# Two decay tiles in SBUF instead of PSUM, in a Mamba and mixture-of-experts kernel

## The reference, cut to what matters

```
dA = exp(dt * A[d, n])
h  = dA * h + dt * B[t, n] * x[t, d]
y[t, d] = sum over n of h[d, n] * C[t, n]
```

## Time and profile before

| | before |
|---|---|
| median of 3 runs | 3176.71 us (3176.48 to 3183.27) |
| the profiled execution | 3177.25 us |
| its span | 3175.4 us |
| mean granted TensorE clock | 0.877 |
| PE busy | 2478.4 us, 78% |
| DVE busy | 2488.7 us, 78% |
| ACT busy | 1384.3 us, 44% |
| POOL busy | 1709.0 us, 54% |

### The profile page before, as it was taken

One profiled execution on the slowest core, in us unless ns is written; L12 is line 12 of the kernel. 1 busy time (PEld: TensorE's weight loads), 2 busy tenths in 40 slices (PEclk: granted clock), 3 DMA queues, 4 the chain that ended last, 5 costly groups with the idle time before them and its releaser, 6 DMA issues.

```text
span 3175.4 us, 35516 instructions
## 1 busy us (share of the span) xinstructions
PE 2478.4 (78%) x10000; PEld 1482.7 (47%) x10000; DVE 2488.7 (78%) x3450; ACT 1384.3 (44%) x2258; POOL 1709.0 (54%) x1290
## 2 busy tenths in 40 slices
PE   5567676697869888697978879697987979687783
PEld 3344444454545455454544545454554545454441
DVE  1888888888888887888888888888978888887202
ACT  2453535354544445354444544354453545432221
POOL 1554656465655656565564756556564656555212
PEclk9778777898979989898998989898998989898987
DMA  2762432223223333333332333333333343333455
GB/s 68 260 241 89 136 103 78 80 93 100 84 80 110 121 99 114 113 107 113 103 120 90 127 106 113 105 101 117 111 112 103 115 128 99 94 113 124 158 185 186
DMA packets 187309, 373.15 MB, mean 118 GB/s; under 512 B 23024, under 2 KB 23024, under 8 KB 187120
## 3 DMA queue, kind: packets, MB, share of 16 engines
q1 hardware_dynamic: 146576, 263.91, 26.2%
q0 software_dynamic: 20480, 67.13, 6.3%
q10 hardware_dynamic: 20064, 39.85, 3.4%
HBM read 212.99 MB, written 157.81 MB: 117 GB/s over the span
## 4 chain that ended last, share of the span: by engine, by line
PE 42%; DVE 27%; issue 14%; POOL 8%; ACT 6%; DMA 3%; DVEq 0%; SPq 0%; POOLq 0%; ACTq 0%
PE work L1011 32%; DVE h L805 10%; DVE acc L819 7%; PE hT L1016 6%; POOL u L557 5%; DVE xc L843 2%; PE work L1016 2%; PE work L1064 2%; ACT decay L690 1%; DMA y_row<-result_scratch,rows_of 1%; DVE acc L816 1%; DVE xc L866 1%; ACT L690 1%; ACT sz L729 1%; DVE shift L884 1%
## 5 line engine op out<-in xcount | busy, mean ns | idle before, releaser
L557 POOL TENSOR_TENSOR u<-xc,b_ring 128x1024 f32<-128x1024 f32 x512 | 1205.0, 2357 | 1057.9 <-DVE h L805 787.0
L690 ACT ACTIVATE decay<-dt,neg_a 128x512 f32<-128x512 f32 x1024 | 705.8, 691 | 1048.9 <-DVE h L805 1035.4
L1016 PE MATMUL hT<-ident,h 128*128 128x128 f32 x4096 | 690.4, 308 | 441.7 <-DVE acc L819 298.3
L819 DVE SCALAR_TENSOR_TENSOR acc<-hT,ct,acc 128x512 f32<-128x512 f32 x960 | 700.2, 730 | 226.8 <-PE hT L1016 200.7
L1016 PEld LDWEIGHTS hT<-ident,h 128*128 128x128 f32 x4096 | 531.3, 158 | 687.7 <-DVE acc L819 388.4
L1011 PE MATMUL work<-w_exp,xeT 128*128 x1536 | 724.4, 616 | 26.7 <-issue 19.1
L805 DVE TENSOR_TENSOR_SCAN h<-decay,h_last,u 128x512 f32<-128x512 f32 x512 | 652.1, 1274 | 44.2 <-ACT decay L690 20.0
L805 DVE TENSOR_TENSOR_SCAN h<-decay,u 128x512 f32<-128x512 f32 x512 | 620.5, 1212 | 57.3 <-ACT decay L690 51.1
L1011 PE MATMUL work<-xnT,w_in 128*128 128x512 f32 x1024 | 476.9, 610 | 0.8 <-ACT xnT L705 0.8
L1011 PEld LDWEIGHTS work<-w_exp,xeT 128*128 128x128 f32 x1536 | 286.1, 196 | 347.1 <-issue 346.7
L1011 PEld LDWEIGHTS work<-xnT,w_in 128*128 128x128 f32 x1024 | 190.5, 196 | 201.3 <-issue 196.2
(11 more groups left out here) (143 smaller groups left out, 1914.6 us busy)
## 6 DMA issues: line engine op xcount, KB each, us to landing
b_ring<-b_scratch SPq DMA_DIRECT2D x256, 256.0 KB
xe<-row_scratch SPq DMA_DIRECT2D x180, 256.0 KB
result_scratch<-ye SPq DMA_DIRECT2D x180, 256.0 KB
row_scratch<-x_out ACTq DMA_DIRECT2D x32, 1024.0 KB, 4.8
xn<-in_x SPq DMA_DIRECT2D x64, 256.0 KB, 4.5
x<-in_x SPq DMA_DIRECT2D x64, 256.0 KB, 5.3
x_scratch<-x SPq DMA_DIRECT2D x64, 256.0 KB, 2.9
x_out<-x_scratch SPq DMA_DIRECT2D x56, 256.0 KB, 3.9
```

The lines of the kernel that those rows point to most:

```text
L557: nc.gpsimd.tensor_tensor(out=u[:, at:at + 2, :], in0=xc[:, half, 2 * k:2 * k + 2, :], in1=b_ring[:, n % ROWS:n % ROWS + 1, :].to_broadcas ...
L690: nc.scalar.activation(decay_bank[g % 2][:], dt[:, half, :], ACT.Exp, scale=neg_a[:, c, n:n + 1]).then_inc(decay_ready, 1)
L819: nc.vector.scalar_tensor_tensor(out=acc[:, q, :], in0=hT_bank[q % 2][:], scalar=ct[:, ip, q, m:m + 1], in1=acc[:, q, :], op0=ALU.mult, op ...
L1016: last = nc.tensor.transpose(ps[:, k * P:(k + 1) * P], tile(k), ident[:])
```

## The change

The two decay tiles are allocated in SBUF, 128 x 512 fp32 each, under the same names. The activation that writes them and the scan that reads them are the same lines with the same waits. The order list is written by another loop: one pass over all 64 places, with constants HT = 2 (number of hT banks) and LAG = 0 (places by which sums are put off), and the sums and transposes come from counts over the whole block. The numbers of the hT banks and the waits on them are written with those counts and have the same values.

The function `transposed_at` gives the transposes of a place. For the sums it yields the places of before. For the transposes of q = 2 and 3 too: behind the sums of q = 0 and 1. Those of q = 0 and 1 of state n come at place 4n + 3, behind its scan and sum and before its side steps; in the list of before they came after these side steps, at the head of state n + 1. For the last state of a block this is the end of the block's own list instead of the head of the next one's.

```diff
@@ -38,6 +38,8 @@
     WORK = 4
+    HT = 2
+    LAG = 0
@@ -122,6 +124,11 @@
+    def transposed_at(at):
+        def last(at):
+            return min(at - C - LAG + HT, (at + 1) // C * C - 1)
+        return range(last(at - 1) + 1, last(at) + 1)
@@ -144,25 +151,24 @@
-        for n in range(N):
-            m, blk = (N - 1, -1) if n == 0 else (n - 1, 0)
-            summing = tail if n == 0 else scan
-            if summing:
-                steps += [("h_T", m, 0, blk), ("h_T", m, 1, blk)]
...
-            for c in range(C):
-                if scan:
-                    steps += [("u", n, c // 2)] * (c % 2 == 0) + [("decay", n, c), ("scan", n, c)]
-                if summing:
-                    steps.append(("h_sum", m, c, blk))
-                    if c + 2 < Q:
-                        steps.append(("h_T", m, c + 2, blk))
...
-                steps += place[n * C + c]
+        for at in range(N * C):
+            n, c = at // C, at % C
...
+            if scan:
+                steps += [("u", n, c // 2)] * (c % 2 == 0) + [("decay", n, c), ("scan", n, c)]
+            k = at - C - LAG
+            if scan if k >= 0 else tail:
+                steps.append(("h_sum", k % (N * Q) // Q, k % Q, k // (N * Q)))
+            for t in transposed_at(at):
+                if scan if t >= 0 else tail:
+                    steps.append(("h_T", t % (N * Q) // Q, t % Q, t // (N * Q)))
...
+            steps += place[at]
@@ -304,8 +310,8 @@
-        decay_bank = [bank(f"decay{i}") for i in range(2)]
-        hT_bank = [bank(f"hT{i}") for i in range(2)]
+        decay_bank = [sb(f"decay{i}", [P, T]) for i in range(2)]
+        hT_bank = [bank(f"hT{i}") for i in range(HT)]
@@ -1024,8 +1031,9 @@
-                        wait(pe, summed, (i * N + m) * Q + q - 1)
-                        transposes(hT_bank[q % 2], lambda k: h[:, m % 2, k, q * P:(q + 1) * P]).then_inc(hT_ready, 1)
+                        k = (i * N + m) * Q + q
+                        wait(pe, summed, k - HT + 1)
+                        transposes(hT_bank[k % HT], lambda k: h[:, m % 2, k, q * P:(q + 1) * P]).then_inc(hT_ready, 1)
```

More of the change, by code:

```diff
@@ L146, in iteration @@
         steps = []
-        for n in range(N):
-            m, blk = (N - 1, -1) if n == 0 else (n - 1, 0)
-            summing = tail if n == 0 else scan
-            if summing:
-                steps += [("h_T", m, 0, blk), ("h_T", m, 1, blk)]
[L152 to L155, removed]
-            for c in range(C):
-                if scan:
-                    steps += [("u", n, c // 2)] * (c % 2 == 0) + [("decay", n, c), ("scan", n, c)]
-                if summing:
-                    steps.append(("h_sum", m, c, blk))
-                    if c + 2 < Q:
-                        steps.append(("h_T", m, c + 2, blk))
-                if scan and j % 2 == 0 and c == 1 and n > 0:
-                    steps.append(("keep_h", n - 1))
-                steps += place[n * C + c]
+        for at in range(N * C):
+            n, c = at // C, at % C
+            if c == 0:
+                if scan and n + 1 < N:
+                    steps.append(("load_b", n + 1, 0))
+                elif do_prep and n + 1 == N:
+                    steps.append(("load_b", 0, 1))
+            if scan:
[6 more added lines that the diff above has]
+                    steps.append(("h_T", t % (N * Q) // Q, t % Q, t // (N * Q)))
+            if scan and j % 2 == 0 and c == 1 and n > 0:
+                steps.append(("keep_h", n - 1))
+            steps += place[at]
         if scan and j % 2 == 0:
@@ L809, in steps_of @@
                         i, ip = j + blk, (j + blk) % 2
-                        dve.wait_ge(hT_ready, (i * N + m) * Q + q + 1)
+                        k = (i * N + m) * Q + q
+                        dve.wait_ge(hT_ready, k + 1)
                         if m == 0:
@@ L815, in steps_of @@
                                     wait_product(dve, j, ("y_T", C - 1))
-                            nc.vector.tensor_scalar(acc[:, q, :], hT_bank[q % 2][:], ct[:, ip, q, m:m + 1], None, ALU.mult).then_inc(summed, 1)
+                            nc.vector.tensor_scalar(acc[:, q, :], hT_bank[k % HT][:], ct[:, ip, q, m:m + 1], None, ALU.mult).then_inc(summed, 1)
                         else:
                             dve.wait_ge(summed, (i * N + m - 1) * Q + q + 1)
-                            nc.vector.scalar_tensor_tensor(out=acc[:, q, :], in0=hT_bank[q % 2][:], scalar=ct[:, ip, q, m:m + 1],
+                            nc.vector.scalar_tensor_tensor(out=acc[:, q, :], in0=hT_bank[k % HT][:], scalar=ct[:, ip, q, m:m + 1],
                                                            in1=acc[:, q, :], op0=ALU.mult, op1=ALU.add).then_inc(summed, 1)
```

## The result

The changed kernel takes 3580.97 us in the median (3575.23 to 3582.18, 4 runs) against 3176.6: 1.1264 times as long, with a 95% interval of 1.1245 to 1.1284, or +404 us. 3570 us were forecast, with a range of 3340 to 3760.

The account below looks back on a forecast made before the run. VectorE and TensorE were each busy 78% of the span, neither alone the bound. Terms 10 + 457 + 15 + 10 + 25 - 150 + 30 = +397 us on 3177 gave 3574, stated as 3570 us, range 3340 to 3760.

Parts of the forecast that it names:

- The write of decay: ScalarE writing the decay tile to SBUF: +15 ns each, at most 15 us, hidden while decays wait for the scan; taken as 0.
- The scan alone: VectorE's scan with both inputs in SBUF: 0 to +20 ns for each of 1024 scans; taken as +10 us.
- The scan stands still for the product: A scan with two SBUF inputs meeting GpSimd's u gets 0.18 us done, stands until u ends, then does the rest.
- How often: Scans meeting GpSimd work: +457 us for first scans during u, +15 gating products, +10 small gate operations, +25 later-starting u.
- the term of late products: 80 u that now start in a scan would start later, by up to 51 us in all, hitting the next scan: +25 us.
- Given back: VectorE's 200.7 us of waits for hT before sums shrink: -150 us; +30 for gaps that leave more of u uncovered.
- its two causes: Later scans make transposes less late; transposes q = 0 and 1 move ahead of TensorE's other steps; together 0 to -200.7 us.
- The sum: All terms added: 10 + 457 + 15 + 10 + 25 - 150 + 30 = +397 us.
- absorbed by 300 us: Rival 1: VectorE's stalls fall into 300 of its 407 us idle time; 3394 us, range 3300 to 3400; chance 13%.
- The convoy: Rival 2: late GpSimd makes u meet the gap inside pairs too, +549 us, nothing given back; about 3830 us; chance 10%.
- a scan that does not stand: Rival 3: the scan does not stand for GpSimd; 3119 us, faster than before; chance 5%.
- a slower TensorE: Lower TensorE clock delaying sums: taken as 0, with up to 50 us of idle time given back left as its price.

Follow-up runs that it names:

- e6: As e5 (u in 2 of 512 columns), with both decay tiles in SBUF, order of before: 3149.92 us, 0.9914 of the kernel before.
- e5: Kernel before, with GpSimd computing u in 2 of its 512 columns except in the first block's first two states: 3102.84 us, 0.9759.
- e3: Kernel before, with only the decay tile of each pair's first scan in SBUF, the second in PSUM: 3457.87 us, 1.0887.
- e4: Kernel before, with only the decay tile of each pair's second scan in SBUF, the first in PSUM: 3248.46 us, 1.0234.
- e7: Changed kernel with each 128x1024 product u as two 128x512 instructions, the scan waiting for the second: 3475.71 us, 1.0933 of the kernel before.
- e1: Changed kernel with both decay tiles back in PSUM, so only the new order of transposes: 3197.24 us, 1.0064 of the kernel before.
- e8: As e1, with a block's second c_project moved from place 39.7 to 38.9, ahead of the moved transposes: 3174.48 us, 0.999 of the kernel before.
- e2: Kernel before, with both decay tiles in SBUF and the order of before: 3569.2 us, 1.1241.
- e9: Kernel before (decay in PSUM, order of before) with each u as two products of 128x512: 3164.26 us, 0.9958.

## Why the prediction was right, point by point

- **The write of decay, 0 us.** The activation takes 721 ns in the mean against 691, +30 ns and not +15. That it is hidden fits the runs: e6, which has it too, is 47 us over e5 with 40 of them in the scans, so at most 7 are left for it.
- **The scan alone, +10 us.** The medians rose by 6 and 10 ns, about 8 us.
- **The scan stands still for the product.** Right in kind: 1.08 us after the product's end is near the 1.24 - 0.18 = 1.06 that the row add's 0.18 us gave. The 1.08 us are the same for scans that take 1.21 us alone and for those that take 1.27, so it is the rest that is fixed, and what gets done beforehand is 0.13 or 0.19 us. e3, e4 and e6 show that it takes both inputs in SBUF and a GpSimd product beside them. The rule of the Trainium skill ("SBUF — State Buffer", "Who interferes with whom") holds for the scan as for the row add, its second half too: a product that comes second stands (2.20 us in e7). Its words that issue order decides who blocks do not fit every case here: 30 scans of the changed kernel begin ahead of the product and stand for it all the same (last section).
- **How often, +457 +15 +10 +25 = +507, with the scan's own 10 = +517.** Measured +549. The +457 for first scans that come while `u` runs was too high: such scans grew by 366 us in the changed kernel. (All first scans together grew by 428, and by 443 in e3.) Too small was the term of late products: the second scans, 93 of which stand, grew by 122 us (99 in e4, where only they can), and I had priced products that slide at 25 us. (The 80 `u` of that term are 42 `u` and 38 gating products in the trace of before.) Left out was a third kind: 30 scans, 16 first and 14 second ones, begin ahead of `u` beside an indirect DMA and stand for the whole of it, 73 us in all. e4 has none of these.
- **Given back, -150 +30.** Waits for hT fell by 172.6 us in the changed kernel, so the size was near. One of its two causes was wrong. I held that the new order of transposes would take up to 135 us; by itself it costs 20 us (e1) and on top of the tiles 12. The transposes of q = 0 are earlier, and TensorE's side steps, and what waits for them, are later (e8 shows it of one step). What gave the time back is that scans come later while TensorE's work stays: -140 us in e2, with the order of before.
- **What I left out.** Waits of scans for decay (+55 us) and for `u` (+36 us) grew, which eats some of what was given back. On the other side some 66 us of other idle time went too, among it 21 us in which the router's `logit` waited for TensorE.
- **The sum.** Busy +549 and idle -148 in the loop make +401; forecast were +517 and -120, +397. The stalls were forecast 32 us too short and what is given back 28 us too small, and the two cancel. That is luck: the 11 us between 3570 and 3581 say less on the working than they seem to.
- **Rivals.** The stall was not absorbed by 300 us (148 were). The convoy's +549 came true in the scans, but not its second half, that nothing is given back. The 390 long scans and e3 refute a scan that does not stand. No cost of a slower TensorE (0.82) shows: the waits for it fell.

## What to carry to other kernels

Before you move an operand of a VectorE instruction from PSUM to SBUF, count the tensors that it then reads from SBUF, and look for GpSimd operations beside it. In this kernel such a pair ran one after the other, and the second lost the rest of the first, though neither waited in any semaphore. (All the GpSimd products here read and write SBUF; which of the two matters was not tried.) The sign is in the spread of durations, not in their medians or in the waits. If one of two buffers must leave PSUM, take the one whose reader mostly comes after GpSimd is done: 71 us against 281 here.

## What the runs showed of the hardware that I had not expected

**A VectorE instruction can miss its turn between two GpSimd instructions.** Of the 285 scans of e7 that begin while a first half runs, 248 go on at its end at the latest, and 37 stand through both. Two row adds of e9, each with GpSimd beside it:

```profile
1269.35 3.11 DVE L995 SCALAR_TENSOR_TENSOR x_out<-y_row,weight_of,x_out 128x512 f32<-128x512 f32 x1
1269.41 1.27 POOL L557 TENSOR_TENSOR u<-xc,b_ring 128x512 f32<-128x512 f32 x1
...
1270.65 1.25 POOL L558 TENSOR_TENSOR u<-xc,b_ring 128x512 f32<-128x512 f32 x1
...
1423.67 1.27 POOL L557 TENSOR_TENSOR u<-xc,b_ring 128x512 f32<-128x512 f32 x1 [0.85 <-DVE h L806]
...
1424.49 1.00 DVE L995 SCALAR_TENSOR_TENSOR x_out<-y_row,weight_of,x_out 128x512 f32<-128x512 f32 x1
1424.89 1.72 POOL L558 TENSOR_TENSOR u<-xc,b_ring 128x512 f32<-128x512 f32 x1
```

The one at 1424.49 comes 0.82 us into the first half, goes on at its end, and the second half stands for it (1.72 us). The one at 1269.35 starts with the first half just about to begin, stands through both (until 1271.90) and ends at 1272.46. In the 10 row adds of e9 over 2.9 us the instruction begins within 0.12 us of a product's start or end, and then misses the next boundary as well. That closeness is of these ten alone: the 37 scans of e7 begin 0.15 to 1.21 us into the first half.

**A scan that begins first can stand, too, when an indirect DMA of GpSimd runs.** Two scans of the changed kernel:

```profile
413.78 1.48 POOL L644 DMA_INDIRECT row_scratch<-x,row_at  x1 [0.30 <-issue]
415.05 3.68 DVE L811 TENSOR_TENSOR_SCAN h<-decay,h_last,u 128x512 f32<-128x512 f32 x1
415.29 2.36 POOL L563 TENSOR_TENSOR u<-xc,b_ring 128x1024 f32<-128x1024 f32 x1
...
2091.87 1.21 DVE L811 TENSOR_TENSOR_SCAN h<-decay,u 128x512 f32<-128x512 f32 x1
2092.23 3.01 POOL L563 TENSOR_TENSOR u<-xc,b_ring 128x1024 f32<-128x1024 f32 x1 [6.15 <-DMA b_ring<-b_scratch]
```

The one at 2091.87 goes through, and the product stands for it (3.01 us in place of 2.36). The one at 415.05 begins 0.23 us ahead of its product, in the last 0.2 us of a DMA, and stands for the whole product. Of the scans that begin 0.2 to 0.4 us ahead of `u`, 29 have a DMA running and all stand, 3 have no GpSimd instruction running and none stands. In e2 it is 35 and 4, in e7 40 and 1. These 29 are all the scans of the changed kernel that take over 3.5 us. Why it is so was not tried.

**GpSimd's indirect DMAs stand for the scan too.** They read their row numbers from SBUF. In the changed kernel:

```profile
L664 POOL DMA_INDIRECT y_row<-result_scratch,rows_of x112 | 163.8, 1463 | 266.6 <-DVE x_out L1001 165.2 <-DVE x L1001 34.4 <-DMA result_scratch<-xn 28.9
```

The mean rose from 1038 to 1463 ns, and that of the scatter from 1003 to 1397. The scatters beside a scan take 1.55 us in the mean, those without one 1.0; in the kernel before, where the scan read PSUM, both kinds took 1.0. The other way round a DMA by itself holds nothing up: all 390 long scans end 1.08 to 1.09 us after a product, and the 65 scans that begin beside a DMA and meet no other GpSimd operation take at most 42 ns more than alone. What it costs a scan is its turn before the next product.
